# Reordering the first phase of a three-layer decoder kernel by deadlines, and splitting the head's weight and row preparation

## The chip, the cores and the metric

One NeuronCore of one Trainium2 chip runs the whole kernel in one launch. The metric is the device time in microseconds (us) of that core. Three runs of the kernel before stand beside one profiled execution.

## The reference

The input is `x` of 8 x 128 x 512 in f32 (8 blocks of 128 tokens, 512 channels) and a context of the same shape. Three layers follow one another, each with a residual and a layer norm ahead of it:

```python
x = x + attn(layernorm(x), Wqkv, bqkv, Wo, bo)                       # one head of 128
x = x + xattn(layernorm(x), ctx, mask, pos_bias, ln_w, w_q, w_k, w_v, w_out)   # 32 heads of 128, keys and values from ctx
x = x + ffn(layernorm(x), base_W, router_W, lora_A, lora_B)          # 8 experts, top 2, low-rank updates
```

`xattn` adds an inner RMS norm with a weight, a positional bias of each head and a key mask, and its own residual.

## The kernel before

Matrix products are taken in f32 by three passes of TensorE over a high and a low part of each operand: `hi*hi + hi*lo + lo*hi`, both parts in the type fp32r. ScalarE (ACT) writes a high part by a cast, VectorE (DVE) the low part by `raw - hi`. A three-pass step of 128x128 by 512 columns is three matmuls, all on line 650.

**The head** (layer 0, about 0 to 75 us). SP's queue loads the blocks of `x`, then the own weights `raw_a`, the context and the first weights of layer 1. DVE takes the statistics of the rows (`row_stats` 1277, `spreads` 1287 to 1300), POOL raises to the power -1/2 (`root`, line 517), DVE writes normalised rows (1304) as it does for all eight blocks, and PE turns them (677 for the first four, 668 for the second four). ACT and DVE split the turned rows into `xt_hi` (988) and `xt_lo` (1325). ACT casts all 1536 columns of the own query, key and value weights in one instruction (1068), and DVE subtracts in one (1435). `project_qkv` then makes queries, keys and values of each half; ACT copies each result out with its bias (`copy_qkv`, 1029); own scores, exponentials, turned probabilities and values (`own_scores`, `exponentials` 1011, `own_probs`, `own_values`, `own_out`) are woven into the first two products of layer 1.

**The first phase** (products 0 to 31, about 43 to 390 us) makes keys and values of layer 1 for 16 pairs of heads from the context by a Strassen-like scheme: each product n has seven slots. A slot needs one combination of context quadrants (`ctx_hi`, `ctx_lo`, seven slots of 128x1024) and one combination of weight quadrants (`w_hi`, `w_lo`). The context's combinations are made once: `ctx_sum` (1420, a subtraction), `ctx_high` (ACT, 1038), `ctx_low` (DVE, 1424). The weights' combinations are made for each product while the one before it runs: `sum_weights` on POOL (536, 538, 544, 545), `high` on ACT (1057, four parts), `low` on DVE (1399, four parts). The results are gathered by `take`: ACT copies four banks into `st` (1065), DVE adds three (1408). PE waits as follows in product n: slot 0 for DVE's three takes of product n-1, slots 2, 3 and 4 for ACT's takes 0, 1 and 2 of this product, slots 5 and 6 for DVE's takes 0 and 1 of this product; and slots 0, 1, 3 and 5 for parts 0 to 3 of `w_lo`. In product 0 alone, each slot also waits for its `ctx_lo`, in the order of the slots.

DVE's order within a product is written out by hand. In an even product from 2 on it first turns the values of the product before (`turn`, 1491, four instructions), then comes `lows` (all four parts), then `takes` (all three):

```python
def keys_taken(k):
    turn(2 * k - 1, k - 1, 1)
    lows(1, k)
    takes(2 * k, 0)
```

An odd product has no turn. ACT's order is high part 0, then take and high in turn, then what stands beside, then its last take. A table `beside` on each engine names other work of layer 0's end and of layer 1's queries, by product: the bias `b_o` added to the residual (`add_b_o` 1528), statistics (`own_stats`), both spreads, `add_normalised` (1316), ACT's `rows_high` (1003) and `take_rows` (996), `x_sum` (1542), `x_high` (1045), `x_lows` (1547), the mask (`masks` 1557, 1560). POOL sums the weights for product n once product n-2 has been finished, and has `root(1, ...)` for both halves behind `sum_for(9)` and `add_mask` (561) behind `sum_for(18)` and `sum_for(20)`.

SP's queue stores and fetches behind semaphores of these steps: a pair's next weights are fetched once the fourth part of `w_lo` has been made; values are stored once turned.

**The second phase** (about 390 to 885 us: 16 pairs of heads, the output projection, layer 2) is not touched.

## Time and profile before

| | |
|---|---|
| median of 3 runs | 885.33 us (884.88 to 886.03) |
| profiled execution, its own time | 887.64 us |
| its span, first to last instruction | 885.9 us |
| PE busy | 848.4 us (96%) |
| DVE busy | 639.6 us (72%) |
| ACT busy | 409.0 us (46%) |
| POOL busy | 358.7 us (40%) |
| DMA | 139.8 MB, 158 GB/s on average |

An engine's busy time is what its instructions cover; the idle time that a timeline row shows in brackets stood just before the row's first instruction, with the work that ended it. A row for x4 merges four instructions: its second number is from the first one's start to the last one's end. Granted clock 1.00 is 2.4 GHz of TensorE and 0.50 is 1.2 GHz.

### The profile page before, as it was taken

To read this page: it belongs to the slowest core of one execution; us is meant where nothing else is said; L and a number is where in the kernel's file an instruction comes from. 1 tells how busy PE (TensorE), PEld (TensorE's weight loads), DVE (VectorE), ACT (ScalarE), POOL (GpSimd) and SP (SyncE) were. 2 spreads that over 40 slices of the span, in tenths; PEclk is the share of its full clock that TensorE was granted. 3 is DMA by queue.
4 is the path that set the end of the run, shared out by engine and by line. 5 is a ranking of instruction groups with operands and counts; after the bars stand their busy time and mean duration, and the time that the engine had idled before them with its cause. 6 is when DMAs were issued, how large, how long until landed. Compare 5 with 4: busy or idle time off the path is not lost.

```text
span 885.9 us, 14164 instructions
## 1 busy us (share of the span) xinstructions
PE 848.4 (96%) x4288; PEld 709.3 (80%) x4288; DVE 639.6 (72%) x1116; ACT 409.0 (46%) x1064; POOL 358.7 (40%) x331
## 2 busy tenths in 40 slices
PE   5789998999999999999999999999999999999898
PEld 4677776887777788787888888888888888888797
DVE  7877776567887766657788777886667866677654
ACT  3453443565433453355455544555345553454220
POOL 2312324223443432235554666545564455643000
PEclk9899999999999999999999999999999999999999
DMA  8026575555666567746777756766566765772002
GB/s 284 2 86 149 136 168 139 142 143 128 169 144 164 142 157 166 143 110 193 219 222 224 204 173 203 197 199 200 171 204 193 202 192 179 205 200 62 1 1 95
DMA packets 231281, 139.78 MB, mean 158 GB/s; under 512 B 139216, under 2 KB 205904, under 8 KB 229328
## 3 DMA queue, kind: packets, MB, share of 16 engines
q1 hardware_dynamic: 231248, 139.38, 57.8%
q8 instruction: 16, 0.26, 0.1%
q14 instruction: 17, 0.14, 0.0%
HBM read 90.07 MB, written 49.28 MB: 157 GB/s over the span
## 4 chain that ended last, share of the span: by engine, by line
PE 81%; DVE 10%; issue 2%; POOL 2%; DMA 2%; ACT 1%; SPq 1%; DVEq 0%; ACTq 0%; POOLq 0%
PE bank L650 66%; PE bank L704 7%; PE bank L789 6%; DVE w_lo L1399 2%; DVE turned L1491 2%; DVE st L1408 1%; DMA values<-turned 1%; PE bank L668 1%; SPq L353 1%; DMA raw_a<-in_w_qkv 1%; POOL w_sum L538 1%; POOL rstd L517 1%; DVE stats L1277 1%; POOL w_sum L536 1%; ACT st L1065 0%
## 5 line engine op out<-in xcount | busy, mean ns | idle before, releaser
L1065 ACT COPY st<-bank 128x512 f32<-128x512 f32 x192 | 112.6, 587 | 245.5 <-PE bank L650 244.6
L650 PE MATMUL bank<-ctx_hi,w_hi 128*128 128x512 f32 x448 | 180.4, 403 | 15.5 <-DVE st L1408 7.4
L650 PE MATMUL bank<-ctx_lo,w_hi 128*128 128x512 f32 x448 | 175.7, 392 | 0.0
L650 PE MATMUL bank<-ctx_hi,w_lo 128*128 128x512 f32 x448 | 175.6, 392 | 0.0
L1408 DVE TENSOR_TENSOR st<-bank,st 128x512 f32<-128x512 f32 x144 | 98.5, 689 | 95.8 <-PE bank L650 95.6
L536 POOL TENSOR_TENSOR w_sum<-raw 128x256 f32<-128x256 f32 x48 | 39.5, 824 | 248.4 <-PE bank L650 226.6
L604 POOL TENSOR_TENSOR weighed<-probs,row_scale 128x512 f32<-128x512 f32 x64 | 70.5, 1107 | 126.4 <-DVE row_scale L1360 125.8
L650 PEld LDWEIGHTS bank<-ctx_hi,w_hi 128*128 128x128 f32 x448 | 84.7, 189 | 45.4 <-issue 10.6
L1011 ACT ACTIVATE probs<-probs,neg_max 128x128 f32<-128x128 f32 x264 | 102.4, 391 | 5.9 <-DVE neg_max L1344 5.9
L1399 DVE TENSOR_TENSOR w_lo<-w_sum,w_hi 128x512 fp32r<-128x512 f32 x96 | 81.8, 862 | 25.3 <-POOL w_sum L544 19.9
L650 PEld LDWEIGHTS bank<-ctx_hi,w_lo 128*128 128x128 f32 x448 | 84.8, 189 | 18.3
L650 PEld LDWEIGHTS bank<-ctx_lo,w_hi 128*128 128x128 f32 x448 | 84.9, 190 | 16.2
L650 PE MATMUL bank<-wo_hi,ot_hi 128*128 128x512 f32 x240 | 95.0, 396 | 0.0
L650 PE MATMUL bank<-wo_hi,ot_lo 128*128 128x512 f32 x240 | 93.6, 390 | 0.0
L650 PE MATMUL bank<-wo_lo,ot_hi 128*128 128x512 f32 x240 | 93.4, 389 | 0.0
L1270 DVE TENSOR_TENSOR acc<-bank,acc 128x512 f32<-128x512 f32 x136 | 89.8, 680 | 3.6 <-PE bank L650 3.6
L650 PE MATMUL bank<-x_hi,w_hi 128*128 128x512 f32 x224 | 89.0, 398 | 0.8 <-ACT st L1065 0.8
L650 PE MATMUL bank<-x_hi,w_lo 128*128 128x512 f32 x224 | 87.5, 390 | 0.0
L650 PE MATMUL bank<-x_lo,w_hi 128*128 128x512 f32 x224 | 87.2, 389 | 0.0
L561 POOL TENSOR_TENSOR bias_mask<-mask_add,bias 128x1024 f32<-128x1024 f32 x32 | 76.7, 2417 | 11.1 <-DVE probs L1339 11.1
L1399 DVE TENSOR_TENSOR w_lo<-raw,w_hi 128x256 fp32r<-128x256 f32 x96 | 60.1, 626 | 23.3 <-ACT w_hi L1057 23.3
L1022 ACT CAST ot_hi<-bank 128x512 fp32r<-128x512 f32 x66 | 38.7, 586 | 75.7 <-PE bank L789 73.2
(148 smaller groups left out, 1507.9 us busy)
## 6 DMA issues: line engine op xcount, KB each, us to landing
raw<-in_weights SPq DMA_DIRECT2D x128, 256.0 KB, 3.6
values<-turned SPq DMA_DIRECT2D x64, 256.0 KB, 4.3
v<-values SPq DMA_DIRECT2D x64, 256.0 KB, 4.8
by_blocks<-probs SPq DMA_DIRECT2D x30, 512.0 KB, 3.2
probs_t<-by_blocks SPq DMA_DIRECT2D x120, 128.0 KB, 2.8
keys<-st SPq DMA_DIRECT2D x14, 1024.0 KB, 5.2
st<-keys SPq DMA_DIRECT2D x28, 512.0 KB, 5.6
acc<-in_x SPq DMA_DIRECT2D x8, 256.0 KB, 6.0
```

The lines of the kernel that those rows point to most:

```text
L536: pool.tensor_tensor(s[:, 1, :], a21, a22, ALU.add).then_inc(w_made[p], 1)
L561: pool.tensor_tensor(bias_mask[j][:, :, :], mask_add[:, :, :], bias[:, j, :].unsqueeze(1).to_broadcast([P, B, P]), ALU.add).then_inc(bias_ ...
L604: pool.tensor_tensor(weighed[i][:, :, :], probs[j][:, half(i), :], row_scale[:, j, half(i)].unsqueeze(2).to_broadcast([P, HALF, P]), ALU.m ...
L650: ins = pe.matmul(out_ap, lhs[a], rhs[b], start=start and k == 0, stop=stop and k == n - 1, skip_group_check=again)
L704: ins = pe.matmul(SC[i][:, cols(t)], q(HALF * i + t), k(HALF * i + t), start=True, stop=True)
L789: ins = pe.matmul(TO[i][:, cols(t)], v[:, j, b, :], probs_t[j][:, :, b, :], start=True, stop=True)
L1011: ins = act.activation(of[:, b, :], of[:, b, :], ACT.Exp, bias=neg_max[:, j, b:b + 1], accum_out=sums[:, j, b:b + 1])
L1022: act.copy(to(i), TO[i][:, :]).then_inc(ot_hi_ready, 1)
L1065: act.copy(to[:, i, j, :], (y, other, y, y)[which][:, :]).then_inc(act_took, 1)
L1270: dve.tensor_tensor(acc[:, b, :], of[:, :], acc[:, b, :], ALU.add).then_inc(out_added, 1)
L1399: dve.tensor_tensor(w[p][1][:, at, :], of, w[p][0][:, at, :].bitcast(F32), ALU.subtract).then_inc(w_lo_ready[p], 1)
L1408: dve.tensor_tensor(to[:, i, j, :], (other, y, other)[which][:, :], to[:, i, j, :], ALU.add).then_inc(dve_took, 1)
```

## The change

It moves work and waits; apart from three small instructions nothing is computed that was not computed before.

- **Head, first rows.** DVE takes the third block's statistics ahead of the first pair's `normalise`, and the first pair's ahead of the fourth block's statistics. The own weights are cast by ACT in three parts and subtracted by DVE in three (`qkv_low`), the first two ahead of the split of the first rows, the third between its second and third chunk. `project_qkv` waits for each part.
- **Head, second rows.** DVE normalises blocks 6 and 7 alone, ACT blocks 4 and 5 (by `shift`, for which POOL makes one more small product, line 525). POOL starts no sum of weights before `xt_lo` of the second rows is complete.
- **Head, order.** On ACT the split of the second rows stands ahead of the value copy; own value turning on PE goes behind the next query projection; the context's highs, lows and sums and the weights' lows are woven between the steps of own attention in the order in which the slots want them. PE takes slot 0 of product 0 ahead of the second turn of values.
- **Every product from 2 on.** On DVE two `low` parts stand ahead of the first take, one between the first and the second, one between the second and the third.
- **Tables.** The work beside is spread: from DVE's odd products (which are followed by a turn) to even ones, over products 2 to 24 instead of 2 to 21; ACT's `x_highs` over 13 to 19 instead of 13 to 17. POOL's `root(1, ...)` stands behind `sum_for(10)`. The loops written as `Fori` start later by two (DVE) and one (ACT).

```diff
@@ gpsimd
-                if layer:
+                if layer or h == half(1):
...
             root(0, half(1), spans(0, 1))
+
+            pool.wait_ge(xt_lo_ready, 2 * KC)
             sum_weights(0, 0)
...
-                if n == 9:
+                if n == 10:
                     root(1, half(0), spans(1, 0))
                     root(1, half(1), spans(1, 1))
@@ tensor
                 if layer == 2:
-                    pe.wait_ge(rows_ready_v, i + 1)
+                    pe.wait_ge(rows_ready_v, i + 2)
+                elif layer == 0:
+                    pe.wait_ge(rows_ready_v, 1)
...
                     n = 3 * i + part
+                    pe.wait_ge(w_qkv_lo_ready, part + 1)
...
-            pe.wait_ge(w_qkv_lo_ready, 1)
             project_qkv(0)
             turn_rows(0, 1)
+            project_qkv(1, (0,))
             turn_values(0)
-            project_qkv(1, (0,))
             pe.wait_ge(xt_lo_ready, 2 * KC)
             own_scores(0)
             project_qkv(1, (1, 2))
             pe.wait_ge(qkv_copied, 5)
             own_scores(1)
+            project_ctx(0, (0,), follow=ctx_lo_ready)
             turn_values(1)
-            pe.wait_ge(qkv_copied, 6)
-            project_ctx(0, (0, 1, 2), follow=ctx_lo_ready)
+            project_ctx(0, (1, 2), follow=ctx_lo_ready)
@@ scalar
-            act.copy(wq[0][:, QKV_COLS], raw_a[:, QKV_COLS]).then_inc(w_qkv_hi_ready, 1)
+            for part in range(3):
+                act.copy(w_qkv_s[0][:, :, cols(part)], raw_qkv_s[:, :, cols(part)]).then_inc(w_qkv_hi_ready, 1)
             split_rows(0, 0)
-            act.wait_ge(raw_o_loaded, 16)
-            act.copy(wq[0][:, OUT_COLS], raw_a[:, OUT_COLS]).then_inc(w_o_hi_ready, 1)
             act.wait_ge(small_loaded, 32)
             copy_qkv(0, 0)
             ctx_high(0)
+            act.wait_ge(raw_o_loaded, 16)
+            act.copy(wq[0][:, OUT_COLS], raw_a[:, OUT_COLS]).then_inc(w_o_hi_ready, 1)
             copy_qkv(0, 1)
             ctx_high(1)
+            normalise(0, 1, (4, 5))
+            split_rows(0, 1)
             act.wait_ge(rows_t_done, 2 * KC)
             copy_qkv(0, 2)
-            split_rows(0, 1)
             ctx_high(3)
+            ctx_high(2)
             copy_qkv(1, 0)
-            ctx_high(2)
             high(0, 0, 0)
+            ctx_high(4)
             exponentials(0, 0, probs0, 0)
+            copy_qkv(1, 1)
             high(0, 0, 1)
-            copy_qkv(1, 1)
             high(0, 0, 2)
             high(0, 0, 3)
+            ctx_high(5)
             copy_qkv(1, 2)
-            ctx_high(4)
             exponentials(0, 0, probs0, 1)
-            ctx_high(5)
             take(0, 0, st[0])
...
-            beside = {9: rows_high(0), 10: rows_high(1), 11: take_rows(0), 12: take_rows(1), 13: x_highs(0, 3),
-                      14: x_highs(5, 1), 15: x_highs(4), 16: x_highs(2), 17: x_highs(6)}
+            beside = {9: rows_high(0), 10: rows_high(1), 11: take_rows(0), 12: take_rows(1), 13: x_highs(0, 3),
+                      14: x_highs(5), 15: x_highs(1), 17: x_highs(4), 18: x_highs(2), 19: x_highs(6)}
@@ vector
-            split_rows(0, 0)
+            row_stats(0, 0); row_stats(0, 1); spreads(0, slice(0, 2)); row_stats(0, 2)
+            normalise(slice(0, 2), 1)
+            row_stats(0, 3); spreads(0, slice(2, HALF)); normalise(slice(2, HALF), 2)
+            qkv_low(0); qkv_low(1); split_rows(0, 0, (0, 1)); qkv_low(2); split_rows(0, 0, (2, 3))
             for b in range(HALF, B):
                 row_stats(0, b)
             spreads(0, half(1))
             ctx_sum(0)
-            normalise(half(1), spans(0, 1))
-            ctx_sum(1); ctx_sum(2); ctx_low(0); split_rows(0, 1); ctx_sum(3)
+            normalise(slice(6, B), spans(0, 1), rows_ready_v)
+            ctx_low(0); ctx_sum(1); split_rows(0, 1); ctx_low(1); ctx_sum(2)
             own_scores(0); maxima(0, 0, probs0, 0); copy_values(0)
-            ctx_low(1); ctx_low(2); own_probs(0); low(0, 0, 0); low(0, 0, 1)
-            own_scores(1); maxima(0, 0, probs0, 1); copy_values(1)
-            low(0, 0, 2); low(0, 0, 3); ctx_low(3); ctx_low(4); own_probs(1); ctx_low(5)
+            low(0, 0, 0); ctx_sum(3); ctx_low(2); low(0, 0, 1); own_probs(0)
+            own_scores(1); maxima(0, 0, probs0, 1)
+            ctx_low(3); low(0, 0, 2); ctx_low(4); copy_values(1); own_probs(1); low(0, 0, 3); ctx_low(5)
...
-            def takes(n, of, odd=False):
-                for which in range(3):
-                    take(n, which, st[of], odd)
+            def takes(n, of, p, m, odd=False):
+                low(p, m, 0)
+                low(p, m, 1)
+                take(n, 0, st[of], odd)
+                low(p, m, 2)
+                take(n, 1, st[of], odd)
+                low(p, m, 3)
+                take(n, 2, st[of], odd)
...
-            beside = {2: add_b_o(0, 1), 3: add_b_o(2, 3, 4, 5), 4: add_b_o(6, 7), 5: own_stats(0, 1, 2),
-                      6: own_stats(3), 7: own_stats(4, 5, 6, 7), 8: both_spreads, 11: add_normalised(0),
-                      13: x_sum(0, 1, 2), 14: x_sum(3), 15: add_normalised(1), 16: masks(0), 17: x_lows(0, 3),
-                      18: masks(1), 19: x_lows(5, 1), 20: x_lows(4), 21: x_lows(2, 6)}
+            beside = {2: add_b_o(0, 1), 3: add_b_o(2), 4: add_b_o(3, 4, 5, 6), 5: add_b_o(7),
+                      6: own_stats(0, 1, 2, 3, 4), 7: own_stats(5), 8: own_stats(6, 7) and both_spreads,
+                      10: add_normalised(0), 12: add_normalised(1), 14: x_sum(0, 1), 16: masks(0) and x_sum(2, 3),
+                      18: x_lows(0, 3), 20: x_lows(5, 1), 22: x_lows(4) and masks(1), 24: x_lows(2, 6)}
```

(The tables and DVE's lists are set here in fewer lines than in the code.)

## Rows read from the trace of the kernel before

**Rows 1.** Windows: length, each engine's busy time (instructions), granted clock, DMA share, GB/s

```profile
0.00:75.22 75.22, 56.98 (x260) 46.62 (x261) 58.19 (x90) 33.19 (x64) 18.85 (x27) 0.95 0.33 116
145.20:161.40 16.20, 12.57 (x44) 9.81 (x43) 6.93 (x20) 7.03 (x12) 6.84 (x10) 0.79 0.47 144
```

**Rows 2.** Waits of PE, whole span: us in total, times, longest

```profile
PE bank L650 <- ACT st L1065: 7.4, 5, 3.6
PE bank L650 <- DVE st L1408: 7.4, 11, 1.1
```

**Rows 3.** Timeline of the first rows: start, us, engine, line, what

```profile
6.14 0.71 POOL L517 TENSOR_TENSOR rstd<-spread,minus_half 128x2 f32<-128x2 f32 x1 [4.09 <-DVE spread L1293]
...
9.66 3.65 PE L677 MATMUL bank<-ident,rows 128*128 128x128 f32 x16 [9.66 <-DVE rows L1304]
...
10.98 1.76 DVE L1435 TENSOR_TENSOR wq_lo<-raw_a,wq_hi 128x1536 fp32r<-128x1536 f32 x1 [0.33 <-ACT wq_hi L1068]
...
12.69 2.48 DVE L1325 TENSOR_TENSOR xt_lo<-bank,xt_hi 128x512 fp32r<-128x512 f32 x4
...
13.53 0.76 PE L650 MATMUL bank<-xt_hi,wq_hi 128*128 128x512 f32 x1 [0.22 <-DVE xt_lo L1325]
```

**Rows 4.** Timeline of the second rows, 18 to 31 us

```profile
18.32 1.91 POOL L517 TENSOR_TENSOR rstd<-spread,minus_half 128x4 f32<-128x4 f32 x1 [8.71 <-DVE spread L1293]
...
20.27 3.58 DVE L1304 TENSOR_SCALAR rows<-acc,mean_var,rstd 128x512 f32<-128x512 f32 x4 [0.90 <-POOL rstd L517]
...
23.90 1.97 PE L668 MATMUL bank<-ident,rows 128*128 128x128 f32 x16 [1.02 <-DVE rows L1304]
...
26.50 2.05 ACT L988 ACTIVATE xt_hi<-bank 128x512 fp32r<-128x512 f32 x4
...
27.65 1.74 DVE L1424 TENSOR_TENSOR ctx_lo<-ctx_raw,ctx_hi 128x1024 fp32r<-128x1024 f32 x1
...
30.14 0.77 PE L650 MATMUL bank<-xt_hi,wq_hi 128*128 128x512 f32 x1 [2.82 <-DVE xt_lo L1325]
```

**Rows 5.** Timeline of PE and DVE, 31 to 76 us

```profile
31.70 1.21 DVE L1420 TENSOR_TENSOR ctx_raw<-ctx_raw 128x1024 f32<-128x1024 f32 x1
...
43.41 0.48 PE L650 MATMUL bank<-ctx_hi,w_hi 128*128 128x512 f32 x1
...
47.72 0.50 PE L650 MATMUL bank<-ctx_hi,w_hi 128*128 128x512 f32 x1 [1.33 <-ACT st L1065]
...
58.16 0.50 PE L650 MATMUL bank<-ctx_hi,w_hi 128*128 128x512 f32 x1 [1.51 <-DVE w_lo L1399]
...
75.22 0.47 PE L650 MATMUL bank<-ctx_hi,w_hi 128*128 128x512 f32 x1 [0.90 <-DVE st L1408]
```

**Rows 6.** Group of the page: busy, mean ns of one, idle before

```profile
L1011 ACT ACTIVATE probs<-probs,neg_max 128x128 f32<-128x128 f32 x264 | 102.4, 391 | 5.9 <-DVE neg_max L1344 5.9
```

**Rows 7.** Timeline around product 9: POOL, ACT, PE

```profile
147.92 1.64 POOL L517 TENSOR_TENSOR rstd<-spread,minus_half 128x8 f32<-128x8 f32 x1
...
150.87 0.72 POOL L538 TENSOR_TENSOR w_sum<-w_sum,raw 128x256 f32<-128x256 f32 x1
...
152.87 0.76 PE L650 MATMUL bank<-ctx_hi,w_hi 128*128 128x512 f32 x1 [3.63 <-ACT st L1065]
```

**Rows 8.** Timelines of DVE and POOL, products 4, 14 and 17

```profile
97.69 2.48 DVE L1491 STREAM_TRANSPOSE turned<-st 128x512 f32<-128x512 f32 x4
...
202.85 4.58 DVE L1542 TENSOR_TENSOR x_raw<-x_raw 128x1024 f32<-128x1024 f32 x3
...
238.89 2.85 POOL L561 TENSOR_TENSOR bias_mask<-mask_add,bias 128x1024 f32<-128x1024 f32 x1
```

**Rows 9.** Timeline: third takes of DVE four products apart, and PE's last such stall

```profile
306.71 0.69 DVE L1408 TENSOR_TENSOR st<-bank,st 128x512 f32<-128x512 f32 x1 [0.77 <-PE bank L650]
...
345.20 0.69 DVE L1408 TENSOR_TENSOR st<-bank,st 128x512 f32<-128x512 f32 x1 [0.77 <-PE bank L650]
...
373.41 0.47 PE L650 MATMUL bank<-ctx_hi,w_hi 128*128 128x512 f32 x1 [0.82 <-DVE st L1408]
```

More of the change, by code:

```diff
@@ L1299, in spreads, with normalise @@
                 ins.then_inc(spread_ready, 1)
-            def normalise(h, count):
+            def normalise(h, count, signal=rows_ready):
                 dve.wait_ge(rstd_ready, count)
@@ L1425, in ctx_low, with qkv_low @@
                                   tok[OF_CTX][0][:, slot, :, :].bitcast(F32), ALU.subtract).then_inc(ctx_lo_ready, 1)
[L1427 to L1437 removed]
+            def qkv_low(part):
+                dve.wait_ge(w_qkv_hi_ready, part + 1)
+                dve.tensor_tensor(w_qkv_s[1][:, :, cols(part)], raw_qkv_s[:, :, cols(part)],
+                                  w_qkv_s[0][:, :, cols(part)].bitcast(F32), ALU.subtract).then_inc(w_qkv_lo_ready, 1)
+            row_stats(0, 0)
+            row_stats(0, 1)
+            spreads(0, slice(0, 2))
+            row_stats(0, 2)
+            normalise(slice(0, 2), 1)
+            row_stats(0, 3)
+            spreads(0, slice(2, HALF))
+            normalise(slice(2, HALF), 2)
+            qkv_low(0)
+            qkv_low(1)
+            split_rows(0, 0, (0, 1))
+            qkv_low(2)
+            split_rows(0, 0, (2, 3))
             for b in range(HALF, B):
@@ L1441, in _ @@
             ctx_sum(0)
-            normalise(half(1), spans(0, 1))
+            normalise(slice(6, B), spans(0, 1), rows_ready_v)
+            ctx_low(0)
             ctx_sum(1)
+            split_rows(0, 1)
+            ctx_low(1)
             ctx_sum(2)
-            ctx_low(0)
-            split_rows(0, 1)
-            ctx_sum(3)
             def copy_values(i):
@@ L1455, in _ @@
             copy_values(0)
-            ctx_low(1)
+            low(0, 0, 0)
+            ctx_sum(3)
             ctx_low(2)
+            low(0, 0, 1)
             own_probs(0)
-            low(0, 0, 0)
-            low(0, 0, 1)
             own_scores(1)
             maxima(0, 0, probs0, 1)
+            ctx_low(3)
+            low(0, 0, 2)
+            ctx_low(4)
             copy_values(1)
-            low(0, 0, 2)
+            own_probs(1)
             low(0, 0, 3)
-            ctx_low(3)
-            ctx_low(4)
-            own_probs(1)
             ctx_low(5)
@@ L1473, in _ @@
             split_own_out(0)
+            low(1, 0, 0)
             take(0, 2, st[0])
+            low(1, 0, 1)
             copy_probs_t(0, probs0_t)
-            for part in range(4):
-                low(1, 0, part)
+            low(1, 0, 2)
+            low(1, 0, 3)
             split_own_out(1)
@@ L1483, in _ @@
             take(1, 1, st[1], odd=True)
-            for b in range(HALF, B):
-                add_out(0, b, OWN_OUT)
-            for part in range(4):
-                low(0, 1, part)
+            low(0, 1, 0)
+            low(0, 1, 1)
+            add_out(0, 4, OWN_OUT)
+            add_out(0, 5, OWN_OUT)
             take(1, 2, st[1], odd=True)
+            low(0, 1, 2)
+            low(0, 1, 3)
+            add_out(0, 6, OWN_OUT)
+            add_out(0, 7, OWN_OUT)
             def turn_blocks(of, i, j):
@@ L1506, in turn @@
                 turn_blocks(of, 1, 0)
-            def lows(p, m):
-                for part in range(4):
-                    low(p, m, part)
-            def takes(n, of, odd=False):
-                for which in range(3):
-                    take(n, which, st[of], odd)
+            def takes(n, of, p, m, odd=False):
[6 more added lines that the diff above has]
+                take(n, 2, st[of], odd)
             def keys_taken(k):
                 turn(2 * k - 1, k - 1, 1)
-                lows(1, k)
-                takes(2 * k, 0)
+                takes(2 * k, 0, 1, k)
             def values_taken(k):
-                lows(0, k + 1)
-                takes(2 * k + 1, 1, odd=True)
+                takes(2 * k + 1, 1, 0, k + 1, odd=True)
             def add_b_o(*some):
@@ L1575, in _ @@
                         beside[n]()
-            with dve.Fori(11, GROUPS - 2) as k:
+                    elif n == 8:
+                        own_stats(6, 7)
+                        both_spreads()
+                    elif n == 16:
+                        masks(0)
+                        x_sum(2, 3)
+                    elif n == 22:
+                        x_lows(4)
+                        masks(1)
+            with dve.Fori(13, GROUPS - 2) as k:
                 keys_taken(k)
@@ L1579, in _ @@
             turn(V1 - 1, GROUPS - 3, 1)
-            lows(1, V0 // 2)
-            takes(V1, 0)
+            takes(V1, 0, 1, V0 // 2)
             turn(V1, GROUPS - 2, 0)
-            lows(0, K0 // 2)
-            takes(V0, 1, odd=True)
+            takes(V0, 1, 0, K0 // 2, odd=True)
             turn(V0, GROUPS - 1, 1)
-            lows(1, Q0 // 2)
-            takes(K0, 0)
-            lows(0, K1 // 2)
-            takes(Q0, 1, odd=True)
+            takes(K0, 0, 1, Q0 // 2)
+            takes(Q0, 1, 0, K1 // 2, odd=True)
             def low_for_queries(g, part):
```

35 lines of the change are left out of this document (12 added, 23 removed).

## The prediction

> **What bounds the kernel now.** I read the page first: PE is busy in 96% of the span, so every gain has to come from stretches in which PE waits or runs slowly. The windows place them: up to 75.22 us PE is busy for 56.98 us, and in 145.20 to 161.40 it is granted 0.79 of its clock [rows 1]. The table of waits then names who ends PE's idle time: ScalarE's takes 7.4 us in 5 waits, VectorE's takes 7.4 us in 11 waits [rows 2]; nearly all lie ahead of 400 us, where the change is made. Last I read the timelines of these stretches, engine by engine [rows 3 to 5, 7 to 9]. From 400 us on nothing in the code changes and I count it at nothing.
>
> First the yardstick. Third takes four products apart start at 306.71 and 345.20 us [rows 9], with no stall of PE between: 9.62 us a product of seven slots. From product 2 (75.22) [rows 5] to slot 5 of product 30 (373.41) [rows 9] lie 28 products, five slots (6.9) and two turnings of rows (1.9 each, as 1.97 in [rows 4]): 269.4 + 6.9 + 3.8 = 280.1 us. It took 298.2. So **18.1 us are lost in the products**, and what of the head can be saved shows in how much earlier than 75.22 product 2 begins.
>
> **The products.** (a) Product 9 is the largest single loss. POOL does both roots (the second from 147.92) ahead of its sums, the second sum of weights begins at 150.87, ScalarE's cast and take stand behind it, and PE idles 3.63 us [rows 7]. Afterwards the clock is low: 0.21 of 16.2 us is 3.4 us [rows 1]. The change puts the roots behind the next sums: four sums of about 0.8 take POOL to 3.1 us into product 9, two roots with their small products (2.1 each) to 7.3 us, and the next sums are wanted at 9.62. ScalarE's `rows_high(0)`, which wants the first root at 5.3, still ends near 8.4, ahead of its last take. All 7.0 us go.
>
> (b) VectorE's takes end the other stalls, 7.4 us less the 0.90 ahead of product 2 [rows 2, 5]. In an even product the turn (2.48) [rows 8], four lows (2.3) and whatever stands beside come ahead of the first take. From the third take of the product before, VectorE is free 0.65 us ahead of the product's start and must have taken by slot 5, 6.87 us in: 6.8 us of room. 4.8 are used, so 2.0 are left, and the work beside doesn't fit: three `x_sum` ahead of product 14's turn took 4.58 [rows 8]. The change puts only two lows ahead of the first take (1.0 instead of 2.3) and nearly all work beside ahead of products without a turn: room is then 5.8 us, and the longest piece, `own_stats` with spreads or the mask with `x_sum`, is about 3.7. In the odd products 17 and 19 POOL's mask, 2.85 us [rows 8], fell on the lows. There too the first take now stands ahead of the low that collides.
>
> The last of them (0.82, product 30) [rows 9] follows a turn that waits for a DMA; the turn stays late, but 1.3 us less stands behind it. All 6.5 us go.
>
> (c) 18.1 - 7.0 - 6.5 leaves 4.6 us. Ten restarts at about 0.3 (the first matmul after a stall is slower, and idle time is counted from a modelled end) are 3.0; the rest is one of ScalarE's smaller waits [rows 2], in product 14, behind the same `x_sum`, and an uneven pace.
>
> The price: the fourth low now waits for slot 4, about 8.2 us into a product instead of 5, and SP's queue fetches the next weights behind it, with value and key stores behind that. SP was busy with stores until nearly then, and the weights are wanted a whole product later: nothing, and if that cover failed, it would be the wait of rival 3. The first extra product written out costs nothing. `x_sum` and `x_lows` beside POOL's sums still delay ScalarE's high parts in products 15, 17, 19 and 21: I leave 0.5 us each. **Products: 18.1 - 2.0 = 16.1 us gained**; ends: 12 (a new stall of 1 us in four products) and 18.
>
> **The head, step by step.** First rows: the first pair's root ends at 6.85 [rows 3], so its two normalisations (0.55 each) end at 7.9 instead of waiting for the fourth block. PE's first eight transposes run from 7.9. The fourth block's statistics and root follow, the second pair is ready near 10.9, PE turns it until 12.6 (13.3 now) [rows 3]. Two parts of the weights' low (0.60 each, a third of 1.76 and a start) and the first split chunk end near 12.9, so the first projection starts at about 13.0 instead of 13.53 [rows 3]. PE is then slow, as it is now in its first five microseconds, so **0.3** are left at the projection's end. If each of three parts costs more than a third, bounds are 0 and 0.6.
>
> Second rows: the root (1.91) starts at 18.4; its extra product for the shift adds 0.3. With POOL waiting, VectorE's two rows take 1.1 us instead of 3.58 for four [rows 4], ready at 21.6. ScalarE's two come behind its second query copy and a context cast, from 21.7, at up to 0.75 each: ready at 23.2. PE turns from 23.2 instead of 23.90 [rows 4]. The splits follow each chunk: ScalarE from 23.8 (2.05 for four) [rows 4], VectorE from 24.4. The next projection starts behind the turning, at 25.2, instead of 30.14 [rows 4], and at the full clock, as only 0.7 us idle stand before it. Now all the idle time from 25.9 to 30.1 and a stretch at 0.43 a matmul instead of 0.23 lie here. PE reaches the context product at 35.7 instead of 43.41 [rows 5], **7.7 ahead**.
>
> Then VectorE is the bound. From 26.8 on: `ctx_low` and `ctx_sum` at 1.74 beside POOL (1.21 alone) [rows 4, 5], to 30.1; own scores, maxima, value copy (0.6 to 0.7 each), low 0, to 32.4; `ctx_sum`, `ctx_low` again at 1.74, low 1, own probabilities, to 37.4; second scores and maxima to 38.8. ScalarE's exponentials (4 x 0.391 and accumulator reads, 1.7) [rows 6] end at 40.5, and only then comes its take, which slot 2 needs: PE goes on at 41.05 after 2.2 us of idle, against 47.72 with 1.33 [rows 5]. I take POOL as busy beside all four big operations; if beside none, take 2 us off; if they cost 2.3 like the slowest, add 2. From slot 2 PE needs what it needs now (47.72 to 56.5 for slots 2 to 6, turns and own values): 49.9. VectorE reaches its third take at 48.8 and has the first lows of the other weights by 48.3 and 49.4, so the 1.51 stall at 58.16 is gone [rows 5]. Product 1 with own outputs took 58.16 to 75.22 less 1.06 for its last stall; product 2 starts at 49.9 + 16.0 = **65.9 instead of 75.22: 9.3 gained**. Ends: 11.5 (no POOL beside) and 4.
>
> A rule that bears on the splitting: TensorE: Matmul & The Clock Gate, Part 1 of the Trainium skill, says the default state is the throttled one and activity releases it. Here a 3.63 us idle time is followed by 0.79 of the clock [rows 1, 7], whereas 1.33 and 1.51 are not followed by slow matmuls [rows 5]; 2.2 lies between. By the rule alone, which names idleness as what brings the slow clock back, one more slow stretch of 3.4 us could follow at 41 us, and the gain would be 22.0; by the nearer rows it isn't. That is rival 1.
>
> **Sum.** 16.1 + 9.3 = 25.4 us. From the profiled execution, 887.64 (span 885.9 and 1.7 around it), that leaves 862.2; this execution stands 2.3 above the median, and against the median 885.33 it is 859.9. I say **860.0**.
>
> **Rivals.** (1) *The idle time moves to slot 2 of product 0 and the clock falls there.* For: VectorE's chain is full from 26.8 to 48.8 and POOL's sums fall into it. Against: the idle time is shorter than both that were followed by a slow clock here. Price: 3.4, and 1 more of idle time: 864.4. Chance 0.16.
> (2) *The tables only move the stalls.* VectorE has 3.7 us pieces ahead of odd products, in which ScalarE's takes hang on POOL's sums, and both slow each other: POOL's mask took 2.85 there, `ctx_low` 1.74 instead of 1.21 [rows 4, 5, 8]. For: such a take of ScalarE's stalled PE in product 14. Against: the pieces are shorter than there. At 1 us in eight products: 868. Chance 0.09.
> (3) *The late fourth low starves the weights, and the kernel is slower.* `low` part 3 frees SP's fetch; if the next weights land after POOL wants them, every product waits. For: the fetch stands in a queue with four stores of values. Against: they have about 9 us after landing. It decides when the wait per product exceeds 25.4/30 = 0.85 us; at 1.2 it is 36 us against 25.4: 896. Chance 0.02.
> (4) *The head gains little*, since ScalarE's rows come last and VectorE's chain is longer than walked: 4 instead of 9.3, 865.3. Chance 0.07.
> My forecast has 0.66.
>
> **The numbers.** Best ends together are 11.5 + 18 = 29.5, 855.8. At the other end the forecast's own range, 856 to 863, is widened over rivals 1 and 4 and most of 2: 855.5 to 868. Within 0.2% (1.8 us, about what a measurement can tell from no change) nothing but a rival 2 of three times the size ends: faster 0.97, same 0.01, slower 0.02.
>
> **What would show it.** Product 2 starts at 65 to 67 us; the second projection's first half starts at 25.2 with no idle time of PE over 1 us until 38; slot 2 of product 0 waits for ScalarE by 1 to 3 us; no wait of PE over 1 us between products 2 and 30, VectorE's takes under 1.5 us in all; clock 1.00 around product 9, where POOL's roots stand behind four sums. The forecast is wrong if `w_made` or `raw` ends PE's waits in every product, if the windows show a low clock between 40 and 60 us, or if PE's waits at slots 3 to 6 come back in the odd products.

## The result, and the profile after

The changed kernel takes 861.02 us (median of 4 runs, 860.05 to 862.2) against 885.68 us for the kernel before (median of 4 runs): 24.7 us less, ratio 0.972 with a 95% interval of 0.971 to 0.974. The forecast was 860.0, with a range of 855.5 to 868.

The windows of the kernel after, cut at product 2 and at the end of the products (length, each engine's busy time with its instructions, granted clock, DMA share, GB/s):

```profile
0.00:67.82 67.82, 55.36 (x261) 45.62 (x262) 53.87 (x86) 34.02 (x66) 19.88 (x26) 0.97 0.38 128
137.00:154.00 17.00, 17.00 (x85) 14.31 (x84) 12.61 (x28) 12.34 (x22) 8.88 (x12) 1.00 0.66 159
154.00:366.00 212.00, 211.52 (x947) 173.04 (x946) 162.91 (x223) 102.62 (x188) 76.82 (x87) 1.00 0.67 161
```

Where PE had waited and run slowly around product 9 [rows 1], it is now busy for all 17.0 us at the full clock, and in the 212 us that follow it is idle for 0.5. The table of PE's waits, whole span (total, times, longest), no longer has VectorE's takes at all, which had ended 11 waits [rows 2]. Two of its rows:

```profile
PE bank L682 <- DVE rows L1311: 9.0, 2, 8.0
PE bank L653 <- ACT st L1070: 4.9, 4, 2.7
```

The head after, timeline of PE (line 653 is the old 650, 1070 the old 1065):

```profile
8.02 1.94 PE L682 MATMUL bank<-ident,rows 128*128 128x128 f32 x8 [8.02 <-DVE rows L1311]
10.90 1.97 PE L682 MATMUL bank<-ident,rows 128*128 128x128 f32 x8 [0.94 <-DVE rows L1311]
13.09 0.77 PE L653 MATMUL bank<-xt_hi,wq_hi 128*128 128x512 f32 x1 [0.22 <-DVE xt_lo L1332]
...
22.79 1.97 PE L673 MATMUL bank<-ident,rows 128*128 128x128 f32 x16 [0.42 <-ACT rows L1008]
24.95 0.47 PE L653 MATMUL bank<-xt_hi,wq_hi 128*128 128x512 f32 x1 [0.20 <-DVE xt_lo L1332]
...
41.54 0.50 PE L653 MATMUL bank<-ctx_hi,w_hi 128*128 128x512 f32 x1 [2.66 <-ACT st L1070]
...
67.80 0.39 PE L653 MATMUL bank<-ctx_hi,w_hi 128*128 128x512 f32 x1
```

The second rows' projection, at 30.14 before [rows 4], starts at 24.95 without a gap. The one wait over 1 us that is left in the head behind 11 us stands at slot 2 of product 0: 2.66 us. Product 2 starts at 67.80 us instead of 75.22 [rows 5].

**Where the time went.** In the two profiled executions the span falls from 885.9 to 858.3, by 27.6 us. ScalarE's fourth take marks the end of each product; its start lies at 365.83 and 341.34 us for product 29, and product 30 takes 10.60 and 9.52, so product 30 ends 25.6 us earlier. Of these 7.4 lie ahead of product 2's start (75.22 and 67.80) and 18.2 behind it; the last 2.0 of the 27.6 us lie behind the products, where no code changed. Of these 2.0, 1.7 are a stretch at half clock (3.4 us long) in the last layer, 838.1 to 841.5 us, that one execution had and the other had not. The windows show both, before and then after:

```profile
836.00:842.00 6.00, 3.61 (x20) 3.64 (x20) 4.88 (x9) 3.42 (x6) 0.67 (x2) 0.72 0.00 0
```

```profile
809.00:815.00 6.00, 3.36 (x28) 2.76 (x26) 5.66 (x10) 3.58 (x6) 1.21 (x2) 1.00 0.00 0
```

That stretch is most of why the span fell by more than the median.

The length of each product, from one fourth take's start to the next, is the measure that the experiments rest on. A product without any stall takes 9.52 us and one with a turning of rows (10 and 12) 11.28; what stands above, summed over products 2 to 30, is lost. (The wait of 0.90 ahead of product 2 counts here to product 2, so that 22.5 less 3.3 is 19.2 and not 18.2.)

```
                products 2 to 30 lose   where (us above 9.52, or above 11.28)
before          22.5   9: 6.7   14: 2.5   4: 1.6   17, 19: 1.3 each   2: 1.3   30: 1.1   16, 18, 20, 22: 0.9 each   8: 0.5   all others 0.10 to 0.25
after            3.3   17: 1.1   19: 0.5   5, 15, 21, 25: 0.4 each
after_again      3.9   the same, and 30: 0.7
b_root          16.6   14: 2.6   30: 1.8   4: 1.6   17, 19: 1.3 each ...
b_takes         10.6   9: 6.3   14: 1.3   2: 1.2   4, 18, 20, 22: 0.4 each
b_tables        17.0   17: 4.6 (1.7 of it slow clock)   19: 2.5   2: 1.3   30: 1.0   5, 15, 21, 25: 0.9 each   9: 0.8 ...
b_head          20.4   9: 6.4   14: 2.5   4: 1.6   17: 1.4   19: 1.3 ...
a_tables_old     3.8   14: 1.3   30: 0.6   4, 18, 20, 22: 0.4 each   16: 0.3
a_singles        0.4   30: 0.4
best             0.0
best_again       0.7   30: 0.6
```

Each line is of one profiled execution. Product 30, whose turn waits for a DMA, differs from one execution to the next of the same kernel: 0.0 and 0.7 in the kernel after, 0.0 and 0.6 in best. So a difference of some 0.7 us that lies in product 30 alone says nothing of an edit.

### The profile page after: what moved, and what is told of

Same layout as the page of the kernel before. It is cut to its first block, busy times and chain, and to the rows that moved or that the text cites. A ratio compares the mean times of both kernels' runs of the same rounds, so it can differ in the third digit from the quotient of the medians.

```text
span 858.3 us, 14107 instructions
## 1 busy us (share of the span) xinstructions
PE 837.1 (98%) x4288; PEld 706.8 (82%) x4288; DVE 646.4 (75%) x1116; ACT 410.5 (48%) x1068; POOL 363.3 (42%) x332
## 4 chain that ended last, share of the span: by engine, by line
PE 93%; DVE 4%; ACT 2%; POOL 1%; issue 0%; DMA 0%; POOLq 0%
PE bank L653 78%; PE bank L795 7%; PE bank L710 7%; PE bank L673 1%; DVE ctx_raw L1427 0%; DVE xt_lo L1332 0%; DVE stats L1284 0%; DMA acc<-in_x 0%; ACT probs L1016 0%; DVE ctx_lo L1431 0%; DVE acc L1771 0%; POOL w_sum L537 0%; POOL w_sum L539 0%; ACT st L1070 0%; POOL rstd L518 0%
## 5 line engine op out<-in xcount | busy, mean ns | idle before, releaser
L653 PE MATMUL bank<-ctx_hi,w_hi 128*128 128x512 f32 x448 | 177.3, 396 | 4.2 <-ACT st L1070 4.1
L653 PEld LDWEIGHTS bank<-ctx_lo,w_hi 128*128 128x128 f32 x448 | 84.4, 188 | 16.6
L1406 DVE TENSOR_TENSOR w_lo<-w_sum,w_hi 128x512 fp32r<-128x512 f32 x96 | 83.9, 874 | 10.3 <-POOL w_sum L545 7.2
L1406 DVE TENSOR_TENSOR w_lo<-raw,w_hi 128x256 fp32r<-128x256 f32 x96 | 67.7, 706 | 3.6 <-ACT w_hi L1062 3.6
```

The source lines that it names most:

```text
L653: ins = pe.matmul(out_ap, lhs[a], rhs[b], start=start and k == 0, stop=stop and k == n - 1, skip_group_check=again)
L1406: dve.tensor_tensor(w[p][1][:, at, :], of, w[p][0][:, at, :].bitcast(F32), ALU.subtract).then_inc(w_lo_ready[p], 1)
```

## The experiments

### One part at a time on the kernel before

b_root moves the root alone, b_takes weaves the lows alone, everywhere (part of its diff):

```diff
-                if n == 9:
+                if n == 10:
```

```diff
...
-                lows(1, k)
-                takes(2 * k, 0)
+                takes(2 * k, 0, 1, k)
...
+                low(p, m, 0)
+                low(p, m, 1)
+                take(n, 0, st[of], odd)
+                low(p, m, 2)
+                take(n, 1, st[of], odd)
+                low(p, m, 3)
+                take(n, 2, st[of], odd)
```

b_tables is b_root with both tables of work beside (VectorE, ScalarE) as the change has them; some lines of VectorE's:

```diff
...
-                      8: both_spreads, 11: lambda: add_normalised(0), 13: lambda: x_sum(0, 1, 2),
+                      10: lambda: add_normalised(0), 12: lambda: add_normalised(1), 14: lambda: x_sum(0, 1),
...
+                    elif n == 16:
+                        masks(0)
+                        x_sum(2, 3)
...
```

b_head is the change without its tables, its takes and its root; against the kernel after, in the even products:

```diff
...
-                takes(2 * k, 0, 1, k)
+                lows(1, k)
+                takes(2 * k, 0)
...
```

> The kernel before with POOL's root(1, ...) behind sum_for(10) and nothing else. Theory (queue order): the whole loss of product 9 goes, 3.6 us of idle time and 3.4 us of slow clock, 7.0 us in all, about 878.5; the clock stays 1.00 from 140 to 165 us. Rival (another wait takes its place, such as ScalarE's rows waiting for the roots): 3.6 us or less, 882 or more, with a new wait of PE in product 9 or 10.

> The kernel before with the four lows woven between VectorE's takes and nothing else. Theory (order within a product): nearly all waits for VectorE's takes go, 6.5 us and their restarts, about 8.5 us in all, 877; product 9 keeps its 3.6 us stall and slow clock. Rival 1 (the tables were what mattered): 3 us or less, 882.5. Rival 2 (the late fourth low starves the weights): slower than before.

> The kernel before with the new tables of work beside on VectorE and ScalarE and with the root moved, lows still first. Theory: 7.0 us from the root, and all stalls for VectorE's takes but those of POOL's mask in products 17 and 19 and of the late turn in product 30 (3.5 us with restarts): 14 us in all, 871.5. Rival (the order within the product was what mattered): 7 to 9 us, 877 to 878.5, with stalls in even products.

> The kernel before with the change's head alone (weights in three parts, rows shared, POOL held back, orders), with the old tables, old order of lows and takes, old place of the root. Theory (the head's gain stands by itself): product 2 starts near 67.8 us instead of 75.22, 7.4 us, about 878. Rival (an earlier head is given back by stalls of the old tables, since what they wait for, such as b_o or the mask, comes by DMA): under 5 us, over 880.5.

Measured, on one chip with the kernel before at 887.2 us:

```
b_root     882.09 us   ratio 0.993 (0.990 to 0.995)    6.3 us by the ratio
b_takes    875.25 us   ratio 0.987 (0.985 to 0.989)   11.2 us
b_tables   878.22 us   ratio 0.990 (0.988 to 0.992)    8.6 us
b_head     879.37 us   ratio 0.992 (0.989 to 0.994)    7.5 us
```

The three parts root, woven lows and head give 6.3 + 11.2 + 7.5 = 25.0 us one by one, and the whole change gives 24.7. Each part is known to about 2 us, so nothing is left over for the tables that could be measured here.

**b_root** holds by its theory: product 9 goes from 16.2 to 9.67 us. The time alone would leave 4 to 8.5 us; its five runs spread from 879.45 to 888.69 us. POOL's timeline shows it, product 9 starting at 146.3 us; the roots stand behind four sums, and the next sum waits for PE instead of PE for it:

```profile
148.79 0.74 POOL L545 TENSOR_TENSOR w_sum<-raw 128x256 f32<-128x256 f32 x1
149.48 1.91 POOL L517 TENSOR_TENSOR rstd<-spread,minus_half 128x8 f32<-128x8 f32 x1
...
156.06 0.73 POOL L536 TENSOR_TENSOR w_sum<-raw 128x256 f32<-128x256 f32 x1 [1.61 <-PE bank L650]
```

The profiled execution of this kernel says nothing of it by its span (887.0), since it ran its last layer at half clock for 13.6 us (835.8 to 849.5); the products' lengths do. It was the longest such stretch of all profiled executions.

**b_takes** gains more than its theory, 11.2 against 8.5 us, and the waits say which ones went; ScalarE's stay, with the 3.6 of product 9:

```profile
PE bank L650 <- ACT st L1065: 7.4, 5, 3.6
...
PE bank L650 <- DVE st L1408: 0.9, 1, 0.9
```

The 0.9 left is the one ahead of product 2, which belongs to the head. The surplus fits the 0.10 us of *every* product. Before, ScalarE's third takes of products 26 and 27 start at 331.31 and 340.94, 9.63 apart:

```profile
331.31 0.59 ACT L1065 COPY st<-bank 128x512 f32<-128x512 f32 x1
...
340.94 0.59 ACT L1065 COPY st<-bank 128x512 f32<-128x512 f32 x1 [0.24 <-PE bank L650]
```

and in b_takes the third takes of products 25 and 26 lie 9.52 apart:

```profile
310.33 0.59 ACT L1065 COPY st<-bank 128x512 f32<-128x512 f32 x1
...
319.85 0.59 ACT L1065 COPY st<-bank 128x512 f32<-128x512 f32 x1
```

PE's own row shows no idle time there in either kernel, so a stretch that looked undisturbed held a small loss 28 times over. The row of PE's weight loads does show it. In product 26 of the kernel before, the load for slot 5 waits for VectorE's first take:

```profile
333.79 0.19 PEld L650 LDWEIGHTS bank<-ctx_hi,w_hi 128*128 128x128 f32 x1 [0.23 <-DVE st L1408]
```

The slot's second matmul then starts 0.305 us after its first instead of 0.227, and the next few are a little late too: 0.10 us in all. In b_takes the loads at this slot wait for nothing, and all 42 matmuls of a product start 0.227 us apart, which makes 9.52.

**b_tables** is far from its theory's 14 us; the rival's number holds (8.6 us, 878.22), but the large stalls stand in odd products and not in even ones. With b_root it shares the root, which alone saves 5.9 us of the products' loss; with the tables added the loss is 17.0 instead of 16.6. Of these 17.0, 1.7 are a stretch at half clock in product 17 (238.2 to 241.6 us). Without it the loss is 15.3, and 0.8 of what is then gained on b_root lies in product 30. So with lows still first the new tables bring 0.5 us, or 1.3 with product 30, where their theory had 7. What they save in even products they lose in odd ones: `masks` and two `x_sum` ahead of product 17 push two lows into POOL's mask, and product 17 loses 2.9 us besides the slow clock, instead of 1.3. VectorE and POOL in product 17:

```profile
231.84 3.94 DVE L1399 TENSOR_TENSOR w_lo<-w_sum,w_hi 128x512 fp32r<-128x512 f32 x2 [0.71 <-POOL w_sum L544]
235.70 0.68 DVE L1399 TENSOR_TENSOR w_lo<-raw,w_hi 128x512 fp32r<-128x512 f32 x1
236.30 1.27 DVE L1408 TENSOR_TENSOR st<-bank,st 128x512 f32<-128x512 f32 x2
```

```profile
232.37 2.86 POOL L561 TENSOR_TENSOR bias_mask<-mask_add,bias 128x1024 f32<-128x1024 f32 x1
```

The first take starts at 236.3, behind all four lows, of which the mask slowed two. PE waits for it, and the clock falls a microsecond later (wait, and window of 235 to 242 us):

```profile
237.03 0.50 PE L650 MATMUL bank<-ctx_hi,w_hi 128*128 128x512 f32 x1 [1.77 <-DVE st L1408]
```

```profile
235.00:242.00 7.00, 5.23 (x17) 3.95 (x16) 5.17 (x8) 0.42 (x2) 0.58 (x2) 0.76 0.24 75
```

This is the collision that the woven order avoids: fewer lows stand ahead of the first take, and in the kernel after no wait of PE for VectorE's takes is left.

**b_head** holds: product 1 ends at 67.71 us instead of 74.36, and 7.5 us of the time are saved; the later products give none of it back (they lose 20.4 us, against 22.5 before).

### Parts taken out of, and added to, the kernel after

a_tables_old is the kernel after with both tables of before. a_take_early moves ScalarE's first two takes of product 0 ahead of the second exponentials and the last context cast:

```diff
-            exponentials(0, 0, probs0, 1)
             take(0, 0, st[0])
-            ctx_high(6)
             take(0, 1, st[0])
+            exponentials(0, 0, probs0, 1)
+            ctx_high(6)
```

a_singles spreads VectorE's table so that two operations with two SBUF operands seldom follow one another, and moves the masks to products 16 and 25, and some of the statistics and `add_b_o` with them; best is a_take_early and a_singles together. Part of a_singles' diff:

```diff
...
-                      5: lambda: add_b_o(7), 6: lambda: own_stats(0, 1, 2, 3, 4), 7: lambda: own_stats(5),
-                      10: lambda: add_normalised(0), 12: lambda: add_normalised(1), 14: lambda: x_sum(0, 1),
-                      18: lambda: x_lows(0, 3), 20: lambda: x_lows(5, 1), 24: lambda: x_lows(2, 6)}
+                      7: lambda: own_stats(3), 10: lambda: add_normalised(0), 12: lambda: add_normalised(1),
+                      13: lambda: x_sum(0), 14: lambda: x_sum(1), 15: lambda: x_sum(2), 16: lambda: masks(0),
+                      17: lambda: x_sum(3), 18: lambda: x_lows(0), 19: lambda: x_lows(3), 20: lambda: x_lows(5),
+                      21: lambda: x_lows(1), 22: lambda: x_lows(4), 23: lambda: x_lows(2), 24: lambda: x_lows(6),
+                      25: lambda: masks(1)}
...
```

> The changed kernel with the old tables of work beside on VectorE and ScalarE; woven lows and the moved root stay. Theory after the first four runs (root, woven takes and head account for the whole gain, the new tables for nothing): 861, within 1 us of the changed kernel; stalls move from products 5, 15, 17, 19, 21 and 25 to 4, 14, 18, 20 and 22. Rival (the tables are worth something once the order is right): 2 us or more slower, 863 or above.

> The changed kernel with ScalarE's first two takes of product 0 ahead of the second exponentials. Theory (slot 2 waits only because the take stands behind the exponentials, and VectorE's chain allows 2 us): PE's wait of 2.7 us at slot 2 breaks into two of about 1 us, product 1 starts 2 us earlier and no slow clock follows: 2 to 3.8 us faster, 858. Rival (VectorE's chain is the bound, its takes come when they come): the idle time reappears whole at slots 3 and 5, under 1 us faster.

> The changed kernel with another table on VectorE: never more than one operation with two SBUF operands of 1024 columns (or two of 512) beside a product, x_sum over products 13 to 17, x_lows one by one over 18 to 24. Theory (what is left in products 5, 15, 17, 19, 21 and 25, 2.8 us, is VectorE and POOL slowing each other when two such operations stand in a row): all of it goes, 858. Rival (some extra work ahead of a turn stalls again, in odd products' successors): 0 to 1 us, 860.5.

> Both together: a_take_early's order on ScalarE and a_singles' table. Theory (they touch different products, so the gains add): 4.8 to 6.6 us faster than the changed kernel, 855.5. Rival (one of them doesn't hold): 858.

Measured on one chip, before at 887.11 us:

```
a_tables_old   862.16 us   ratio 0.971 (0.969 to 0.974)
a_take_early   861.15 us   ratio 0.971 (0.969 to 0.973)
a_singles      860.90 us   ratio 0.971 (0.968 to 0.974)
best           857.16 us   ratio 0.966 (0.963 to 0.968)
```

The changed kernel's own ratio, 0.972 to 0.973 in its two measurements, lies inside the intervals of the first three, so the times alone decide none of them, and the theories' 858 us for a_take_early and a_singles is not what their medians show; the traces say more. **a_tables_old** loses 3.8 us in the products against 3.3, and the 0.5 between them lies in product 30: in products 2 to 29 both lose 3.2 to 3.3, at different places. So with woven lows the new tables are worth nothing that the runs show, and the theory formed after the first four runs holds. **a_singles** takes 9.52 us for every product from 2 to 29 but the two with rows (11.28). Three of its six runs took 858.8 to 858.9 us and three 862.9 to 865.1, the latter at a lower mean granted clock (0.99 against 0.998), which is why its median doesn't show the gain.

What was left came from operations with two SBUF operands in a row. In the kernel after, `x_sum` and `x_lows` stand in five pairs ahead of products 15, 17, 19, 21 and 25, and each time the second of the pair takes 1.64 to 1.77 us beside a POOL sum of 1.60; alone they take 1.22 and 0.74. In a_singles all eleven take 1.22, and no sum of weights in products 2 to 30 takes over 1.3. In product 17 of the kernel after, VectorE's second `x_sum` and POOL's second sum slow each other (1.64 and 1.60), ScalarE's cast waits 1.42 us for that sum, and its take comes late:

```profile
216.28 1.64 DVE L1563 TENSOR_TENSOR x_raw<-x_raw 128x1024 f32<-128x1024 f32 x1
216.91 1.60 POOL L539 TENSOR_TENSOR w_sum<-w_sum,raw 128x256 f32<-128x256 f32 x1
...
218.55 0.62 ACT L1062 CAST w_hi<-w_sum 128x512 fp32r<-128x512 f32 x1 [1.42 <-POOL w_sum L539]
...
219.07 0.58 ACT L1070 COPY st<-bank 128x512 f32<-128x512 f32 x1
```

A single `x_sum` in a_singles:

```profile
223.23 1.22 DVE L1563 TENSOR_TENSOR x_raw<-x_raw 128x1024 f32<-128x1024 f32 x1
```

**a_take_early** ends product 1 at 65.76 instead of 68.00 us, 2.2 us earlier as its theory has it, but most of that is clock. The idle time of 2.66 us becomes two of 0.46 and 0.98, and no slow clock follows:

```profile
41.10 0.50 PE L653 MATMUL bank<-ctx_hi,w_hi 128*128 128x512 f32 x1 [0.46 <-DVE w_lo L1406]
46.03 0.47 PE L653 MATMUL bank<-ctx_hi,w_hi 128*128 128x512 f32 x1 [0.98 <-DVE st L1415]
```

Now VectorE ends both waits: its chain is the bound of the head. How much is order and how much clock shows from the start of the second rows' turning to the end of product 1. It is 43.0 us in all three profiled executions with early takes (a_take_early, best, best_again), 43.6 in the two of the old order without a slow stretch (after_again, b_head), and 45.2 to 45.5 in the three with one of 3.4 us (after, a_tables_old, a_singles). So the order itself gives 0.6 us; the rest comes from the slow clock, which four of six executions with the long wait had and none of the three with early takes.

**best** takes 857.16 us, nearer its rival's 858 than its theory's 855.5; by the ratios it is some 6 us faster than the changed kernel, which was not measured on the same chip. In it PE is busy in all of 270 us:

```profile
67.00:337.00 270.00, 270.00 (x1209) 224.06 (x1208) 206.25 (x319) 137.68 (x247) 98.67 (x120) 1.00 0.69 164
```

### A check on one chip, and two parts of the head

a_poolfree takes away POOL's added wait; a_alldve gives ScalarE's two second rows back to VectorE:

```diff
-            pool.wait_ge(xt_lo_ready, 2 * KC)
```

```diff
-            normalise(0, 1, (4, 5))
...
+            normalise(slice(HALF, 6), spans(0, 1))
```

> The changed kernel unaltered, so that the others of this call have it on the same chip: 24 to 25 us faster than before, 0.972.

> The version with early takes and single operations once more, beside the changed kernel on one chip. Theory (the two gains add, 2.3 us in the head with its slow clock and 2.9 in the products): 5 us faster than the changed kernel, ratio to before 0.966. Rival (the difference was one between chips): under 2 us.

> The changed kernel without POOL's wait for xt_lo. Theory (POOL's sums slow VectorE wherever they fall, and held back they fall into VectorE's full chain): rows and the first context steps slower by about 2 us, PE's second rows 0.8 us later, but the chain after 27 us shorter; in all within 1 us of the changed kernel, product 2 at 67 to 68.5 us. Rival (holding POOL back carries the head's gain): product 2 at 70 us or later, 2 us or more slower.

> The changed kernel with all four second rows normalised by VectorE and none by ScalarE. Theory (the sharing saves little, since POOL is held back and four rows take 2.0 us there): PE turns the second rows at 22.9 us instead of 23.1 with ScalarE's, context steps on VectorE 1.0 us later, so slot 2 of product 0 at 1 us later: 0.5 to 1.5 us slower. Rival (the sharing is what brings the rows forward): PE turns them a microsecond or more later and the clock falls: 3 us or more slower.

Measured on one chip, before at 886.43 us:

```
after_again   861.68 us   ratio 0.973 (0.971 to 0.976)
best_again    856.77 us   ratio 0.967 (0.965 to 0.968)
a_poolfree    860.11 us   ratio 0.970 (0.968 to 0.972)
a_alldve      863.39 us   ratio 0.975 (0.973 to 0.978)
```

**best_again** repeats: 4.9 us faster than the changed kernel on the same chip, with intervals apart, as its theory has it (5). **a_poolfree** is not slower, so the rival falls: holding POOL back is worth nothing in the time. Product 1 ends at 67.58 us against 67.60. The idle time has only moved from slot 2 of product 0 to the second projection, and the half clock with it (28.1 to 31.5 us):

```profile
26.72 0.47 PE L652 MATMUL bank<-xt_hi,wq_hi 128*128 128x512 f32 x1 [2.04 <-DVE xt_lo L1331]
42.69 0.50 PE L652 MATMUL bank<-ctx_hi,w_hi 128*128 128x512 f32 x1 [0.45 <-ACT st L1069]
```

**a_alldve** ends product 1 at 70.66 us, 3.1 later than after_again, but the times of the two overlap within their intervals (1.7 us apart). Most of the 3.1 is clock. The windows of after_again and a_alldve (same columns as above):

```profile
41.00:49.00 8.00, 6.28 (x34) 5.34 (x34) 7.84 (x11) 5.50 (x16) 0.00 (x0) 1.00 0.19 67
```

```profile
41.00:49.00 8.00, 5.99 (x16) 4.82 (x17) 5.79 (x8) 5.38 (x15) 0.00 (x0) 0.58 0.21 66
```

0.42 of 8 us are 3.4. Slot 2 of product 0 itself is only 0.3 us later (43.01 against 42.72), but after_again is a poor measure for this: its first projection ran slowly for longer than that of the other executions. From 15 to 17 us it has 6 matmuls, the first execution of the same kernel has 11. (The column of the granted clock tells nothing here, since its record begins with the first rise to full, at 17.09 us in after_again and 14.87 in after.) After_again, then after:

```profile
15.00:17.00 2.00, 2.00 (x6) 1.54 (x6) 2.00 (x5) 0.00 (x0) 0.00 (x0) 1.00 1.06 389
```

```profile
15.00:17.00 2.00, 2.00 (x11) 1.60 (x10) 2.00 (x4) 0.00 (x0) 0.00 (x0) 1.00 1.06 382
```

ScalarE's part of the second rows comes behind copies of that projection, so PE turns the rows at 23.97 us there and at 22.79 in after. Counted from the end of POOL's root for the second rows, slot 2 starts 22.1 us later in a_alldve and 21.1 to 21.2 in after, a_singles and a_tables_old, whose first projection ran like its own. So among executions that are alike the sharing with ScalarE is worth some 0.9 us at slot 2, inside its theory's 0.5 to 1.5; after_again's 22.0 us are as long as without it. Whether a slow stretch follows decides more.

## Why the prediction was right

**The sum.** 25.4 us were forecast, 24.7 measured. The head and the products were both found where the prediction looked for them, and both terms were off, in opposite directions: the products gave 18.2 us instead of 16.1, the head 7.4 instead of 9.3. (These two are of the profiled executions, which differ by more than the medians.) That the sum came so near is in part luck: an error of 2.1 us one way met one of 1.9 the other way. The two mechanisms that carry the products, POOL's queue order and the woven lows, are each shown by a run of their own. By one of its own signs the forecast was wrong: it named a low clock between 40 and 60 us, and the profiled execution had one.

**Product 9**, forecast 7.0: measured 6.3 to 6.7 (b_root's time by its ratio; 16.2 to 9.53 in the lengths). Queue order on POOL was the cause, as b_root shows alone. In the kernel after, sums end at 138.3 and both roots at 143.2, and the next sum waits 1.42 us for PE. The roots end some 8.1 us into the product instead of the 7.3 forecast, but the cover that the prediction named is there.

**VectorE's takes.** Forecast: all their waits go. They did in the profile after; in after_again one of 0.44 us is left, in product 30. The step that failed is the yardstick: 9.62 us was taken for an undisturbed product, and 9.52 is; a turning of rows costs 1.76 and not 1.9. With these the same sum gives 21.3 us lost instead of "18.1 us are lost in the products", and the woven order had more to give than it was credited with. (18.2 gained and 3.3 kept are 21.5.) The residue of 2.0 us was low too; 3.3 stayed, in products 5, 15, 17, 19, 21 and 25. The mechanism given for it, `x_sum` and `x_lows` beside POOL's sums, was right for the last five, and a_singles removed it there. Product 5 has neither: four `add_b_o` in a row stand ahead of it, two of which take 1.23 us instead of 0.69 beside POOL sums of 1.07 to 1.09. Its 0.4 us went in a_singles too, which has two in a row there.

**The tables**, which the prediction argued as half of the remedy ("nearly all work beside ahead of products without a turn"), weren't: with woven lows nothing outside product 30 (a_tables_old), with lows first 0.5 to 1.3 us (b_tables against b_root, without the slow stretch). The room argument foresaw fewer stalls in even products, and b_tables has fewer there; it left out what the same work does to the odd products behind it. With the lows woven both tables lose the same 3.2 to 3.3 us in products 2 to 29.

**The head.** The walk held to within half a microsecond as far as slot 2: first projection 13.0 forecast, 13.09 measured; second rows 23.2 and 22.79; next projection 25.2 and 24.95; VectorE's second maxima end 38.8 and 39.3; slot 2 at 41.05 and 41.54. What failed is the term behind it: rival 1 happened in the profiled execution, with the clock at half from 42.17 to 45.59 us, 1.7 us lost, not the 3.4 of its price, and product 1 ends late by that. The wait was 2.66 us and not 2.2. From slot 2 to product 2 the forecast had 24.9 us; 26.3 were measured here, and in after_again, without a slow stretch, 24.7. Here is the stretch:

```profile
41.00:46.00 5.00, 4.46 (x15) 3.60 (x16) 4.32 (x7) 3.67 (x8) 0.00 (x0) 0.66 0.13 43
```

The sentence "by the nearer rows it isn't" doesn't stand: of six profiled executions with 2.65 to 2.95 us of idle time at this place, four (after, a_tables_old, a_singles, a_alldve) were followed by a slow clock, after_again (2.67) and b_head (2.65) were not. Which of the head's many new orders carries its 7.4 us was taken apart only for the two parts of a_poolfree and a_alldve; for the others, such as the weights in three parts, it stays open.

**The extra wait of POOL** was taken as what makes two rows cost 1.1 instead of 3.58 for four. The row costs are right (1.0 us measured for two, and 0.94 for each row in a_poolfree), and a_poolfree shows that they don't matter to the end of the head. That VectorE pays for POOL's sums once, early or late, fits this but is not shown by itself.

**Rival 3**, the late fourth low, did not occur: in the kernel after no wait of PE of 0.15 us or more is ended by weights in any product.

## What to carry to other kernels

When an engine has both work with a deadline and work that only must be done within the period, put the deadlines' work between the other, and look for a fixed small loss per period by comparing the period with its count of instructions and by the waits of the weight loads, not by PE's idle time. In this kernel, once the order was right, moving work from odd periods to even ones brought nothing; what was left was two engines slowing each other on operations with two SBUF operands, and only spreading these one by one removed it. A change's profile should be read for the stretch at low clock that it does or doesn't have before spans are subtracted.

## What the runs showed that was not expected

A product in which PE shows no wait in the profile was 0.10 us longer than its matmuls need, and all products of the kernel before from 2 on were longer by about that or more. They lost it when VectorE's takes no longer came just in time: the wait stood in the weight load and not in the matmul.

The slow clock after a given idle time is not the same from one execution to the next: after 2.65 and 2.67 us of idle time at slot 2 the clock stayed at 1.00, after 2.66, 2.93 and 2.95 it fell to 0.50 for 3.4 us, and after 2.95 in a_alldve for 6.8. The two that stayed (b_head, after_again) are those whose clock had first risen late, at 17.6 and 17.1 us, the four that fell had it at full from 14.4 to 14.9 us on. The late rise costs over a microsecond of its own: in after_again slot 2 starts 1.2 us later than in after, and product 1 still ends 0.4 us earlier. Shorter waits can be enough: in b_tables the clock fell after 1.77 us in product 17 (with 0.48 us five microseconds ahead) and not after 1.76 in product 19. In the last layer, where no code differs, it was low for 3.4 us in some executions, for 13.6 in b_root, and not at all in others.

The Trainium skill, TensorE: Matmul & The Clock Gate, Part 1, says that the number of slow matmuls at the start differs from one run to the next of the same kernel. The traces agree: 6 against 11 matmuls from 15 to 17 us in two executions of the kernel after.
